# The second feed-forward of a four-layer graph network: where its first bias is added, and which engine normalizes its residual

## What is computed

```
logits = mean(x, axis=1) @ Wr + br                # one row per graph
...                                               # softmax, capacity, softmax again
top_w, top_i = jax.lax.top_k(rw_tok, 2)           # the same two experts for all nodes of a graph
top_w = jax.nn.softmax(top_w, axis=-1)
h = gelu(einsum('nd,edf->enf', xf, W1) + b1[:, None, :], approximate=False)   # 128 -> 256
y = einsum('enf,efd->end', h, W2) + b2[:, None, :]                            # 256 -> 128
out = einsum('ne,end->nd', w_dense, y)
out = layer_norm(out + x, gamma, beta)
```

## Time and profile before

| | us |
|---|---|
| Median of 3 runs | 670.67 (669.17 to 672.07) |
| The profiled execution, its own time | 673.78 |
| Its span, first to last instruction | 672.0 |
| TensorE busy (matmuls), share of the span | 581.3 (87%) |
| VectorE busy | 439.8 (65%) |
| ScalarE busy | 406.7 (61%) |
| GpSimd busy | 237.3 (35%) |
| Last layer: its first `up` product to the end of its last product | 508.78 to 660.42 |

### The profile page before, as it was taken

The page is one execution under the profiler, slowest core; times in us unless marked ns, Lnnn a source line. Parts: engine busy times, 40 slices in busy tenths (PEclk is TensorE's granted clock), DMA queues, the critical chain, the costliest instruction groups (busy, mean ns, idle before and its releaser), DMA issues.

```text
span 672.0 us, 15279 instructions
## 1 busy us (share of the span) xinstructions
PE 581.3 (87%) x4000; PEld 473.0 (70%) x4001; DVE 439.8 (65%) x1648; ACT 406.7 (61%) x974; POOL 237.3 (35%) x461
## 2 busy tenths in 40 slices
PE   3457999999999999999999999987317999999993
PEld 2335777777777777777777776765217999999992
DVE  3456678888788898888888897754250443444435
ACT  1224657868768877777778678665312466555661
POOL 4131223342343433434433432312220344554444
PEclk9999999999999999999999999999656999999997
DMA  8403044042142241350440420330006444445412
GB/s 176 120 0 117 28 141 141 4 142 89 55 141 69 72 141 48 93 141 17 124 139 3 140 95 2 95 98 0 0 0 185 123 139 136 141 141 152 133 43 62
DMA packets 74598, 61.99 MB, mean 92 GB/s; under 512 B 7772, under 2 KB 62268, under 8 KB 74562
## 3 DMA queue, kind: packets, MB, share of 16 engines
q1 hardware_dynamic: 61344, 56.14, 28.2%
q10 hardware_dynamic: 13218, 5.42, 3.2%
HBM read 57.13 MB, written 4.41 MB: 92 GB/s over the span
## 4 chain that ended last, share of the span: by engine, by line
PE 31%; DVE 17%; DMA 15%; issue 14%; ACT 12%; POOL 5%; SPq 4%; DVEq 1%; ACTq 0%; POOLq 0%
DMA x<-in_x 12%; PE bank L1477 5%; PE bank L1490 4%; PE wide L1477 4%; PE wide L1490 4%; SPq L611 4%; ACT p_xn L120 3%; DMA w_scratch<-wrow 3%; PE bank L1300 2%; DVE h2w L994 2%; PE bank L1313 2%; DVE route_stats L88 2%; DVE at_prT L317 2%; ACT h L780 2%; ACT at_lk L284 2%
## 5 line engine op out<-in xcount | busy, mean ns | idle before, releaser
L1313 PE MATMUL bank<-w,h2w 128*128 128x128 f32 x768 | 104.0, 279 | 2.1 <-DVE h2w L994 2.0
L1300 PE MATMUL bank<-h,w 128*128 128x512 f32 x192 | 101.3, 609 | 4.9 <-ACT h L785 4.8
L1313 PEld LDWEIGHTS bank<-w,h2w 128*128 128x128 f32 x768 | 95.6, 193 | 5.5 <-DVE h2w L994 3.1
L780 ACT ACTIVATE h<-bank,b 128x512 f32<-128x512 f32 x96 | 66.4, 691 | 46.8 <-PE bank L1300 46.8
L785 ACT ACTIVATE h<-bank,b 128x512 f32<-128x512 f32 x96 | 66.0, 687 | 29.4 <-PE bank L1294 29.3
L994 DVE TENSOR_TENSOR h2w<-h,wide_w 128x512 f32<-128x512 f32 x96 | 65.0, 677 | 14.9 <-ACT h L780 10.6
L1292 PE MATMUL bank<-xnTh,w1h 128*128 128x512 f32 x96 | 67.8, 707 | 0.0
L101 POOL TENSOR_TENSOR route_var_eps<-route_mean_var,eps 128x4 f32<-128x4 f32 x16 | 10.9, 680 | 124.8 <-DVE route_mean_var L94 124.8
L101 POOL TENSOR_TENSOR at_var_eps<-at_mean_var,eps 128x4 f32<-128x4 f32 x32 | 12.7, 396 | 101.3 <-DVE at_mean_var L94 101.3
L240 PEld LDWEIGHTS wide<-at_wh,at_prT 128*128 128x128 f32 x256 | 33.5, 204 | 17.3 <-issue 7.9
L1235 DVE SCALAR_TENSOR_TENSOR at_y<-bank,gw,at_xT 128x128 f32<-128x128 f32 x32 | 9.0, 345 | 53.0 <-PE bank L1490 53.0
(11 more groups left out here) (233 smaller groups left out, 1464.6 us busy)
## 6 DMA issues: line engine op xcount, KB each, us to landing
wide_w<-w_scratch SPq DMA_DIRECT2D x96, 256.0 KB, 4.5
mask<-in_L_ffn_W SPq DMA_DIRECT2D x128, 128.0 KB, 2.1
x<-in_x SPq DMA_DIRECT2D x16, 256.0 KB, 5.9
xin<-in_x SPq DMA_DIRECT2D x16, 256.0 KB, 6.0
adj_in<-in_adj SPq DMA_DIRECT2D x16, 256.0 KB, 6.5
out<-at_pr ACTq DMA_DIRECT2D x8, 256.0 KB, 3.0
out<-at_prT ACTq DMA_DIRECT2D x8, 256.0 KB, 2.6
W<-in_L_ffn_W SPq DMA_DIRECT2D x2, 512.0 KB
```

Of the source, the lines that this page charges most:

```text
L780: a.activation(h2[:, e % 2, :], b_h2[:, :], ACT.Relu, bias=b2[:, e:e + 1]).then_inc(h2_ready, 1)
L1300: pe.matmul(b_h2[:, :], w2[:, e, :], h1[:, e % 2, :], start=True, stop=True).then_inc(l2_done, 1)
L1313: last = pe.matmul(b_out[:, s], h2w[:, e % 2, s], w3[:, e, :], start=False, stop=(e == E0 - 1), skip_group_check=True)
```

## The change

The first bias is no longer put into the bank by TensorE. Two transposing loads put `b1` into `b1col`, with the hidden feature on the partition and one column for each half and expert. ScalarE reads the group's eight expert numbers into registers and applies four Gelus of 128x128 for each graph in place of one of 128x512, each with the column of its expert as bias. `up` on TensorE is left with the four f32 products, and TensorE reads 8 expert numbers for a group instead of 12 (4 instead of 8 for the first). `b1row` with its zeroing, its split and its way through DRAM is gone. The residual's normalization leaves ScalarE: VectorE does it by four `tensor_scalar` instructions at the start of each of its groups, ahead of `tail_sum` of the group before.

```diff
-    b1row = sb("b1row", [P, E1, FC * P], BF16)
+    b1col = sb("b1col", [P, FC, E1])
-    LATE = 16 * 8
+    LATE = 16 * 9
 # SyncE, load_late
-                sp.dma_start(brsrc[0:E1 * FC, :], A["L1_ffn_b1"].rearrange("e (c p) -> (e c) p", c=FC)).then_inc(late_loaded, 16)
-                sp.dma_start(brsrc[E1 * FC:, :], A["L1_ffn_b2"]).then_inc(late_loaded, 16)
+                    for c in range(FC):
+                        sp.dma_start(b1col[:, c, :], A["L1_ffn_b1"][:, c * P:(c + 1) * P].rearrange("e p -> p e"))\
+                            .then_inc(late_loaded, 16)
+                sp.dma_start(brsrc[:, :], A["L1_ffn_b2"]).then_inc(late_loaded, 16)
 # GpSimd, later_constants
                 p.memset(onesb[:, :], 1.0).then_inc(brow_zero, 1)
-                p.memset(b1row[:, :, :], 0.0).then_inc(brow_zero, 1)
                 p.memset(b2row[:, :, :], 0.0).then_inc(brow_zero, 1)
 # ScalarE
-            def gelus(m, t):
+            def gelus(m, t, experts):
                 a.wait_ge(up_done, m + 1)
                 need(a, down_done, m - 3)
-                a.activation(hid[t][:, :], up_bank[t][:, :], ACT.Gelu).then_inc(gelu_ready, 1)
+                for j in range(2 * FC):
+                    k, c = j // FC, j % FC
+                    s = slice(j * P, (j + 1) * P)
+                    last = a.activation(hid[t][:, s], up_bank[t][:, s], ACT.Gelu,
+                                        bias=b1col[:, c, bass.ds(experts[k], 1)])
+                last.then_inc(gelu_ready, 1)
...
             def group(g, g0, par):
+                picked = chosen(mybir.EngineType.Activation, GG * g, GG)
                 for t in range(GG):
-                    gelus(GG * g + t, t)
-                    if t == 0:
-                        residual(g, par)
+                    gelus(GG * g + t, t, picked[2 * t:2 * t + 2])
...
+            a.wait_ge(gidx_ready, 1)
 # VectorE
+            def residual(g, par):
+                settle(v, const_ready)
+                need(v, sum_ready, g - 1)
+                for q in range(GG):
+                    m = bass.ds(g * GG + q, 1)
+                    last = v.tensor_scalar(res[par][:, q * P:(q + 1) * P], x_tile(g)(q), rstd3[:, m], shift3[:, m],
+                                           ALU.mult, ALU.add)
+                last.then_inc(res_normed, 1)
             def group(g, g0, par):
+                residual(g, par)
                 if g0 > 0:
                     tail_sum(g - 1, 1 - par)
 # TensorE, up
                 need(pe, gelu_ready, m - 3)
-                for j in range(2 * FC):
-                    k, c = j // FC, j % FC
-                    pe.matmul(up_bank[t][:, j * P:(j + 1) * P],
-                              b1row[:, bass.ds(experts[k], 1), c * P:(c + 1) * P].rearrange("p a f -> p (a f)"),
-                              onesb[:, :], start=(j == 0), stop=False, skip_group_check=True)
                 pe.wait_ge(w1_loaded[slot], 16 * g_even + 32)
...
-                                     xnT3[:, bass.ds(m * P, P)], start=False, stop=True, skip_group_check=True)
+                                     xnT3[:, bass.ds(m * P, P)], start=True, stop=True, skip_group_check=True)
 # TensorE, group
-                picked = chosen(mybir.EngineType.PE, GG * g - early, GG + early)
+                picked = chosen(mybir.EngineType.PE, GG * g - early, 2 + early)
```

More of the change, by code:

```diff
@@ L437, in build @@
     fn = norm_stage(nc, "final")
-    brsrc = sb("brsrc", [E1 * FC + E1, P])
-    brpart = sb("brpart", [E1 * FC + E1, 3, P], BF16)
-    brrest = sb("brrest", [E1 * FC + E1, P])
-    b1row = sb("b1row", [P, E1, FC * P], BF16)
+    brsrc = sb("brsrc", [E1, P])
+    brpart = sb("brpart", [E1, 3, P], BF16)
+    brrest = sb("brrest", [E1, P])
+    b1col = sb("b1col", [P, FC, E1])
     b2row = sb("b2row", [P, E1, P], BF16)
@@ L447, in build @@
     w_dram = nc.dram_tensor("w_scratch", (2, E0, GW), F32).ap()
-    br_dram = nc.dram_tensor("br_scratch", (3, (E1 * FC + E1) * P), BF16).ap()
+    br_dram = nc.dram_tensor("br_scratch", (3, E1 * P), BF16).ap()
     hid = [at0["lk"], at0["pr"], p_xn, w2[:, 0:GG, :].rearrange("p a d -> p (a d)")]
@@ L572, in load_late @@
                     sp.dma_start(W2[:, :, c * P:(c + 1) * P], w2d[:, :, c, :]).then_inc(late_loaded, 16)
-                sp.dma_start(brsrc[0:E1 * FC, :], A["L1_ffn_b1"].rearrange("e (c p) -> (e c) p", c=FC)).then_inc(late_loaded, 16)
-                sp.dma_start(brsrc[E1 * FC:, :], A["L1_ffn_b2"]).then_inc(late_loaded, 16)
+                with nc.allow_non_contiguous_dma(reason="bias columns, once"):
+                    for c in range(FC):
+                        sp.dma_start(b1col[:, c, :], A["L1_ffn_b1"][:, c * P:(c + 1) * P].rearrange("e p -> p e"))\
+                            .then_inc(late_loaded, 16)
+                sp.dma_start(brsrc[:, :], A["L1_ffn_b2"]).then_inc(late_loaded, 16)
                 sp.dma_start(wr[:, :], A["L1_ffn_Wr"]).then_inc(late_loaded, 16)
@@ L631, in _ @@
             sp.wait_ge(br_stored, 16)
-            sp.wait_ge(brow_zero, 3)
-            cut = E1 * FC * P
-            sp.dma_start(b1row[0:3, :, :].rearrange("q e f -> q (e f)"), br_dram[:, 0:cut]).then_inc(brow_loaded, 16)
-            sp.dma_start(b2row[0:3, :, :].rearrange("q e f -> q (e f)"), br_dram[:, cut:]).then_inc(brow_loaded, 16)
+            sp.wait_ge(brow_zero, 2)
+            sp.dma_start(b2row[0:3, :, :].rearrange("q e f -> q (e f)"), br_dram[:, :]).then_inc(brow_loaded, 16)
             def load_w1(g, par):
@@ L908, in store @@
                 a.dma_start(dst, tiles(fin[par][:, :])).then_inc(stored[par], 16)
-            def residual(g, par):
-                need(a, sum_ready, g - 1)
-                for q in range(GG):
-                    m = bass.ds(g * GG + q, 1)
-                    last = a.activation(res[par][:, q * P:(q + 1) * P], x_tile(g)(q), ACT.Identity,
-                                        bias=shift3[:, m], scale=rstd3[:, m])
-                last.then_inc(res_normed, 1)
             def group(g, g0, par):
+                picked = chosen(mybir.EngineType.Activation, GG * g, GG)
                 for t in range(GG):
-                    gelus(GG * g + t, t)
-                    if t == 0:
-                        residual(g, par)
+                    gelus(GG * g + t, t, picked[2 * t:2 * t + 2])
                     if t == 1 and g0 > 1:
@@ L1461, in _, with up @@
             pe.wait_ge(gidx_ready, 1)
-            pe.wait_ge(brow_zero, 3)
-            pe.wait_ge(brow_loaded, 32)
-            def up(m, slot, g_even, experts):
+            pe.wait_ge(brow_zero, 2)
+            pe.wait_ge(brow_loaded, 16)
+            def up(m, slot, g_even):
                 t = slot % GG
                 need(pe, gelu_ready, m - 3)
-                for j in range(2 * FC):
-                    k, c = j // FC, j % FC
-                    pe.matmul(up_bank[t][:, j * P:(j + 1) * P],
-                              b1row[:, bass.ds(experts[k], 1), c * P:(c + 1) * P].rearrange("p a f -> p (a f)"),
-                              onesb[:, :], start=(j == 0), stop=False, skip_group_check=True)
                 pe.wait_ge(w1_loaded[slot], 16 * g_even + 32)
@@ L1498, in group @@
                 early = 2 if g0 > 0 else 0
-                picked = chosen(mybir.EngineType.PE, GG * g - early, GG + early)
-                pairs_of = [picked[2 * q:2 * q + 2] for q in range(GG + early)]
+                picked = chosen(mybir.EngineType.PE, GG * g - early, 2 + early)
+                pairs_of = [picked[2 * q:2 * q + 2] for q in range(2 + early)]
                 for t in range(GG):
-                    up(GG * g + t, GG * gpar + t, g_even, pairs_of[t + early])
+                    up(GG * g + t, GG * gpar + t, g_even)
                     if t < 2 and g0 > 0:
```

## The result

The changed kernel takes 647.13 us (median of 4 runs, 646.04 to 649.94) against 671.15 us (669.17 to 672.07) of the kernel before on the same chip: ratio 0.9652, 95% interval 0.9614 to 0.969. A second comparison, on another chip, gave 648.36 us (647.42 to 649.69, 6 runs) against 670.63 (668.71 to 674.37, 11 runs), ratio 0.9661 (0.9637 to 0.9685). So the change saves 22 to 24 us; the forecast was 21.3 us, 649.4.

What follows compares the result with a forecast made beforehand. TensorE's own work bounds the last layer; bias products 17.6, seams 2.0 and memset 1.7 sum to 21.3 us, from 670.7 to 649.4 us (3.2% less), chance 0.86. Range 645.5 to 655.5 us.

Steps and rivals of the forecast that it cites:

- The bound: Last layer: TensorE waits for nothing after the first W1, so work taken from it is worth its full price.
- the rivals: ScalarE slows kernel (0.04); ScalarE paces, still faster (0.06); no effect beyond memset (0.03); VectorE delays sums (0.01).
- Bias products: TensorE, last layer: graphs 3 to 63 each lose 0.28 us, graphs 1 and 2 together 0.5; sum 17.6 us.
- Seams: Begins of groups in TensorE's loop: shorter register load and f32 products behind it gain 2.0 us, between 0 and 2.8.
- Memset: GpSimd's zeroing of b1row delays the second group's split; removal moves the program forward 1.7 us, bounds 0 and 1.8.
- ScalarE: Last layer: four Gelus 1.28 us; a group 7.9 us in series, nearer 6.8, against TensorE's 8.0, so hidden.
- The rival: ScalarE slows the kernel: queue and engine do not overlap, 9.8 us a group, about 674 us; chance 0.04.
- The rule against it: About 200 ns a register: ScalarE's load takes 1.6 us, its group 8.8 us in series, over TensorE's 8.0.
- VectorE: Last layer: the residual's four instructions, 1.11 us, fit in the 4.79 us wait before tail_sum; about 3.4 remain, no cost.
- Loads: Two transposing loads ahead of the third group's x fit in 19 us; W1 loads come faster; cost nothing.
- The end: From the last product on, the chain over VectorE and GpSimd stays unchanged.
- The clock: TensorE's rise to 2.4 GHz, some 6 us after becoming busy, could shift against the work; about 1 us either side.

Runs made afterwards that it cites:

- the timed pair: Kernel before with only b1row's zeroing moved some 3 us earlier, into GpSimd's idle time, against the kernel before: 668.75 us against 670.63.
- The run with eight halves: Changed kernel with eight Gelus of 64 columns a graph instead of four of 128: 650.41 us, 2.0 us over the changed kernel.
- the slowest kernel: Changed kernel with eight Gelus of 64 columns a graph and the residual's normalization back on ScalarE: 673.71 us against 670.51 of the kernel before.
- the edit: Changed kernel with the second bias's products also taken off TensorE: 636.81 us; with its new transfers moved to other queue places, 631.32 us.

## Why the prediction was right, step by step

- **The bound.** Right. TensorE's pace was what the last layer cost, before and after; every run that took work off it returned its price in full, 16.7 of 16.8 us between graph 3 and graph 63 for the bias products alone, and 14.3 in the stage for the second bias. None of the rivals came about by itself.
- **Bias products, 17.6 us.** Right in size: 16.7 us between graph 3 and graph 63, and the way from the first `up` product to that of graph 3 went from 7.58 to 6.67 us, 0.9 instead of the 0.8 forecast (0.5 for the slow start and 0.28 for graph 3's own).
- **Seams, 2.0 of 0 to 2.8.** Inside the range, somewhat small (all 2.6 us went), and the mechanism was half right. I named two causes, the long register load and the short bias products used up behind it. The run without bias products kept all of the seams, so only the load is left of the two; their 0.57 instead of 0.39 us was where the wait showed, not what made it.
- **Memset, 1.7 of 0 to 1.8.** The place was right, the price at or above my upper end: 1.83 us at the split, 1.9 us in the timed pair and 2.3 to 2.9 across chips. I had taken the length of the instruction as the most that it can cost, which leaves out what a shifted start does to the rounds behind; the cause of the surplus is open, and the interval of the pair (0.9 to 3.2 us) would also allow none.
- **ScalarE.** The direction was right, the size too high. I forecast 7.9 us in series and "nearer 6.8"; it is 5.6, since four Gelus cost 1.02 us and neither the register load nor the store's issue is seen on the engine. The edge I gave, 0.40 us a Gelu, fits by the measured pieces: (8.02 - 1.54) / 16 = 0.405. The run with eight halves, 0.39 us for 128 columns, stands just under it and leaves TensorE's steady pace as it was; the one with the residual on top stands over it and gives 673.7 us. The rival had said about 674 for 9.8 us a group; that the numbers meet is in part luck, since its group was made of other pieces and 4.1 us of the time lie behind the last `up`.
- **The rule against it.** The Trainium skill, Runtime: NRT & Kernel Launch, section Instruction fetch mechanics, about 200 ns a register, would have made ScalarE's load of 8 numbers 1.6 us. ScalarE's own row is 0.55 us. The trace does not agree.
- **VectorE.** Right. The wait that covers the residual, 4.79 us before, is 2.40 us now, with the residual ahead of it. Timeline:

```profile
559.92 1.11 DVE L1251 TENSOR_SCALAR at_prT<-x,rstd,shift 128x128 f32 x4
563.43 1.13 DVE L1232 SCALAR_TENSOR_TENSOR at_y<-bank,gw,at_xT 128x128 f32<-128x128 f32 x4 [2.40 <-PE bank L1493]
```

  The forecast was 3.4 us of cover for 1.11 us of residual; 2.40 + 1.11 = 3.5.
- **Loads.** Right. The third group's `x` is issued at 26.45 instead of 23.96 us, lands 4.1 us after that and is first read at 41.5. TensorE waits for no W1 but the first. (The 127 GB/s of the earlier trace rows stand beside 246 and 204 in the stretches around it, which is not less than half; nothing hung on it.)
- **The end.** Unchanged: 8.81 us from the last product to the last store before and after (660.42 to 669.23, 633.69 to 642.50).
- **The clock.** I gave it about 1 us to both sides. In the two traces compared it rose 6.1 and 5.8 us after the first `up` product, so it hardly counted; over all executions it came 3.0 to 6.5 us after, and one stage was 1.7 us shorter by it. That the forecast's pair was so alike is luck.
- **The sum.** 20.3 us in the stage and 1.9 to 2.4 ahead of it make 22.2 to 22.7, the forecast 21.3. The terms that were too low (start 0.1, seams 0.6, memset 0.2 to 0.7) are the difference. The medians differ by 22 to 24, and the first W1 load comes some 4 us earlier in the traces; what of that goes beyond the memset is open.

## What to carry to other kernels

Where one engine sets the pace without a wait, price the removed work at its full length, and look for what it also starved: here 2.6 us lay at the begins of the groups, behind a long register load in the queue of the bound engine. To tell how much an engine can still take, read the distance from start to start of its groups, not the sum of busy times and issues; that is what says how near the next bound is. And before adding transfers, follow the queue that feeds the bound engine: one wait ahead of its loads cost 4.2 us here, 2.6 of standing and 1.6 of the slower clock behind it, over a quarter of what the edit had won.

## What the runs showed of the hardware

- A register load of 8 numbers takes 0.52 us on SyncE, 0.55 on ScalarE, 0.60 on TensorE (medians of the kernel after); one of 4 on TensorE 0.34. The number of registers does not fix it: on TensorE 12 numbers took 0.85 us in the unrolled groups and up to 1.6 in the loop, and 8 numbers 1.1 to 1.3 in the loop of the slowest kernel. What lengthens them isn't settled.
- ScalarE's register loads, register operations and DMA issues take nothing from its computing as long as it is behind: Gelus of 64 columns with a register's address start 0.196 us apart, eight in 1.57 us, right through a register load of 0.55 us.
- The time of a row on ScalarE is not its price when the engine is behind: 128x64 Gelus show a mean of 0.9 to 1.05 us each in the slowest kernel (891 to 1052 ns), started every 0.196 us.
- After the first `up` product the granted clock came to 2.4 GHz 3.0 to 6.5 us later in the thirteen executions of much the same stage (3.0, 3.8, 5.8 and 6.1 in the four named above). Why it differs isn't settled.
- Pauses of TensorE of 1.0 to 1.5 us, one a group in the loop, left the granted clock at 1.00 in the steady part (510.8 to 657.6); after pauses of 1.8 and 2.5 us it fell to 0.50. Windows of the kernel with eight Gelus and the residual on ScalarE, in the steady part and at its end:

```profile
600.00:640.00 40.00, 35.43 (x306) 33.85 (x305) 17.05 (x72) 40.00 (x173) 19.39 (x28) 1.00 0.44 131
...
656.00:657.00 1.00, 0.00 (x0) 0.00 (x0) 0.32 (x1) 1.00 (x11) 0.92 (x3) 1.00 0.00 0
657.00:658.00 1.00, 0.92 (x6) 0.83 (x7) 0.38 (x1) 1.00 (x8) 1.00 (x1) 0.79 0.00 0
658.00:659.00 1.00, 1.00 (x7) 0.91 (x6) 0.00 (x0) 0.74 (x4) 0.84 (x4) 0.50 0.00 0
```
